# Causal attention and a top-1 expert layer on one core: score tiles cut into quarters of queries, and the expert choice made on the activation instead of in the gate product

## The reference, cut to what matters

```python
x = L0_attn_x                                   # (4, 1024, 128), float32
q, k, v = heads_of(layernorm(x) @ W.T + b)      # 16 heads of 8 columns, for Wq, Wk, Wv
scores = q @ k.T / sqrt(8);  scores = where(causal mask, scores, -9e15)
x = x + softmax(scores) @ v @ Wo.T + bo
z = layernorm(x);  logits = z @ gate_w.T        # 8 experts
sel = argmax(logits);  rw = sigmoid(max(logits))
for e in range(8):
    xs = z * (rw * (sel == e))[:, None]
    out += (xs @ w_up[e].T * silu(xs @ w_gate[e].T)) @ w_down[e].T    # 64 inner columns
return x + out
```

## Time and profile before

| | us |
|---|---|
| median of three runs | 563.52 (563.22 to 566.83) |
| the profiled execution | 562.29 |
| its span | 560.6 |
| front, to the loop's first full unit | 68.64 |
| fifteen units | 341.06 |
| last unit | 24.30 |
| expert steps | 126.60 |

### The profile page before, as it was taken

One profiled execution on the slowest core, in us unless ns is written; L12 is line 12 of the kernel. 1 busy time (PEld: TensorE's weight loads), 2 busy tenths in 40 slices (PEclk: granted clock), 3 DMA queues, 4 the chain that ended last, 5 costly groups with the idle time before them and its releaser, 6 DMA issues.

```text
span 560.6 us, 12273 instructions
## 1 busy us (share of the span) xinstructions
PE 533.4 (95%) x4674; PEld 234.5 (42%) x4674; DVE 449.8 (80%) x668; ACT 385.0 (69%) x771; POOL 211.2 (38%) x393
## 2 busy tenths in 40 slices
PE   8559899999999999999999999999988999999996
PEld 6324434333343333433434334334223555666553
DVE  6938899999999999999999999999924655655631
ACT  7224688898998998988989899899886322222221
POOL 5577264443363444533544346314142111111100
PEclk9769999999999999999999999999999999999999
DMA  6151122320211511102232021120030112121000
GB/s 174 30 168 52 37 64 73 111 66 10 65 37 36 168 28 57 56 18 69 80 104 68 10 66 42 43 69 10 7 100 4 48 56 62 56 58 57 19 20 19
DMA packets 27866, 32.45 MB, mean 58 GB/s; under 512 B 4384, under 2 KB 21280, under 8 KB 27808
## 3 DMA queue, kind: packets, MB, share of 16 engines
q1 hardware_dynamic: 27664, 31.28, 19.2%
q10 hardware_dynamic: 144, 0.39, 0.2%
HBM read 20.26 MB, written 11.01 MB: 56 GB/s over the span
## 4 chain that ended last, share of the span: by engine, by line
PE 70%; DVE 18%; ACT 4%; POOL 3%; issue 2%; DMA 2%; ACTq 1%; POOLq 0%; DVEq 0%
PE ps L1062 19%; PE ps L1046 13%; PE ps L1003 8%; DVE top_p L825 7%; DVE top_p L827 6%; PE ps L1115 6%; PE ps L1123 5%; PE ps L1112 5%; ACT prob L681 4%; DVE top_p L820 3%; PE ps L1013 3%; PE ps L947 2%; PE ps L938 2%; PE ps L1113 2%; PE ps L1021 1%
## 5 line engine op out<-in xcount | busy, mean ns | idle before, releaser
L681 ACT ACTIVATE prob<-ps 128x512 f32<-128x512 f32 (+2 forms) x640 | 307.5, 560 | 41.6 <-PE ps L1046 36.8
L827 DVE TENSOR_REDUCE top_p<-ps 128x2 f32<-128x1024 f32 x192 | 223.6, 1217 | 5.4 <-PE ps L1013 1.8
L1046 PE MATMUL ps<-q_rows,k_rows 51*128 51x512 bf16 (+3 forms) x768 | 168.9, 328 | 2.7 <-ACT prob L681 1.4
L1062 PE MATMUL ps<-prob,v_all 128*9 128x512 f32 (+3 forms) x1536 | 156.8, 488 | 0.7 <-ACT sum_sb L672 0.4
L581 POOL TENSOR_SCALAR_AFFINE_SELECT prob<-prob 128x512 f32<-128x512 f32 x128 | 81.4, 636 | 184.8 <-ACT prob L681 183.0
L1003 PE MATMUL ps<-k_rows,q_rows 48*128 48x512 bf16 (+2 forms) x896 | 130.7, 305 | 8.9 <-DMA k_rows<-split_parts 6.9
L1046 PEld LDWEIGHTS ps<-q_rows,k_rows 51*128 51x128 bf16 x768 | 52.4, 93 | 135.4 <-ACT prob L681 120.0
L825 DVE TENSOR_REDUCE top_p<-ps 128x4 f32<-128x1024 f32 x64 | 76.4, 1214 | 3.5 <-PE ps L1013 3.3
L1003 PEld LDWEIGHTS ps<-k_rows,q_rows 48*128 48x128 bf16 x896 | 42.8, 94 | 45.3 <-issue 15.5
L724 ACT ACTIVATE prob<-ps 128x512 f32<-128x512 f32 x32 | 19.1, 597 | 56.0 <-PE ps L1113 56.0
L903 DVE TENSOR_TENSOR prob<-ps,prob 128x512 f32<-128x512 f32 x32 | 22.1, 690 | 36.9 <-PE ps L1115 36.9
(11 more groups left out here) (90 smaller groups left out, 430.1 us busy)
## 6 DMA issues: line engine op xcount, KB each, us to landing
split_parts<-part SPq DMA_DIRECT2D x6, 768.0 KB, 5.1
q_rows<-split_parts SPq DMA_DIRECT2D x31, 96.0 KB
k_rows<-split_parts SPq DMA_DIRECT2D x31, 96.0 KB
value_sums<-sum_sb SPq DMA_DIRECT2D x128, 18.0 KB
x_sb<-x SPq DMA_DIRECT2D x8, 256.0 KB, 4.5
qk<-value_sums SPq DMA_DIRECT2D x8, 256.0 KB, 3.6
qk<-inverse_sums SPq DMA_DIRECT2D x8, 256.0 KB, 3.8
out<-y SPq DMA_DIRECT2D x8, 256.0 KB, 2.3
```

Of the source, the lines that this page charges most:

```text
L681: a.activation(prob[:, i % NB, g0:g0 + heads, 0:cols], ps[:, load_at(u, n) % 3, 0:heads * cols].rearrange("p (s t) -> p s t", s=heads), AC ...
L827: return v.tensor_reduce(top_p[:, place, qt, s:s + 3:2], banks, AX.X, ALU.max)
L1046: last = mm(ps[:, l % 3, m * cols:(m + 1) * cols], k_rows[rows, k, s + m, j * P:(j + 1) * P], q_rows[rows, k, s + m, c * HALF + q0:(c + 1) ...
L1062: last = mm(ps[32 * g:32 * g + HD + 1, BANK_V, q0:HALF], v_all[:, b, j, first_head + g, :], prob[:, i % NB, g, 0:n], start=(j == 0), stop= ...
```

## The change

Two parts of the program are rewritten.

**The loop.** The eight quarters of 64 tokens in each half of a batch are stored in another order (1, 3, 5, 7, 6, 4, 2, 0, done on the inputs before the launch and undone on the output), keys are put back in their natural order when `xn_t` is written, so q is projected in two products. A query tile is now two quarters that do not adjoin: Y tiles are quarters 1, 3 and 5, 7 of a half, X tiles 6, 4 and 2, 0, and a Z tile is one quarter of each kind, its two halves of 64 queries with different keys. There are 17 pieces per unit. A mask is one matmul per bank instead of two. The queries of a slot are still as many, but lie in the middle of the half, and POOL masks two pieces of 64 columns instead of one of 128. The turn is one transpose (48 columns) instead of four, the join two instructions on 64 partitions each. `send_parts` issues two DMAs instead of one, and stands at another place of SP's queue; the expert weights are loaded during unit 2.

**The expert steps.** The chosen expert's rank is spread over all partitions (PE, then a copy by ACT) and DVE compares and multiplies it into the activation (`choose`, four per step); the `shut` products are gone; gates run ahead of the ups; `down` comes in two parts with the spread rank and the turn between them.

```diff
-PIECES = []
-PIECES.append((P, 0, [(qt, s, P * qt, True) for qt in (0, 4) for s in range(2)]))
...
-PIECES += [(HALF, 2, [(qt, s, 0, False)]) for qt in range(4, 8) for s in range(2)]
+PIECES = [("X", Q, [(c, s, m) for c in range(2) for s in range(2) for m in range(2)], 5)]
+for c in range(2):
+    blocks = [(c, s, m) for s in range(2) for m in range(2)]
+    PIECES += [("Y", P, blocks, 3), ("Z", P, blocks, 4)]
+    PIECES += [("X", 2 * P, [(c, s, 0) for s in range(2)], 6), ("Y", 2 * P, [(c, s, 1) for s in range(2)], 2)]
...
+PIECES += [(tile, HALF, [(1, s, m)], place) for m in range(2) for tile, place in (("X", 7), ("Y", 1))
+           for s in range(2)]
...
-ORDER = "PSSPVSSVaSSPSSPSVSSPVSPSSSPSVSSPSPSVVSPSSPVSPSSVbSSPSPVSSSPVSPSSPSSSPSVS"
+ORDER = "SPSPSSVVaVSSPPSSVSSSPVSSPSSPSSVSPSPSSVSPSVSPSSPVSSbSPSPSVSPSSVSSPSPSVSS"
...
 def send_parts(b, h, units=range(UPB)):
...
+                for s in range(2):
+                    sp.dma_start(split[:, :, UPB * b + units.start:UPB * b + units.stop, :, :, h, s, :]
...
 def step(u, between=None):                       # POOL
-                        blockv = prob[:, i % NB, :, 0:P]
-                        g.affine_select(out=blockv, in_=blockv, pattern=[[0, GH], [1, P]], base=0,
...
+                        for z in range(2):
+                            q0 = (SLOTS[i][3] - Q) * z
+                            quarter = prob[:, i % NB, :, q0:q0 + Q]
+                            last = g.affine_select(out=quarter, in_=quarter, pattern=[[0, GH], [1, Q]],
...
 def copy_xn(b, h):                               # ACT
-                a.activation(xn_t[:, h, :], ps[:, bank, :], ACT.Copy).then_inc(xn_t_set[h], 1)
+                tokens = xn_t[:, h, :].rearrange("p (m e t) -> p m e t", e=2, t=Q)
+                a.activation(tokens[:, :, 1, :], ps[:, bank, 0:HALF // 2].rearrange("p (m t) -> p m t", t=Q), ACT.Copy)
+                a.activation(tokens[:, ::-1, 0, :], ps[:, bank, HALF // 2:].rearrange("p (m t) -> p m t", t=Q),
...
 def join(u, c):                                  # DVE
+                for h in range(2):
+                    rows = slice(Q * h, Q * h + Q)
+                    last = v.tensor_reduce(top[rows, c].rearrange("p g (k m) -> p k g m", k=2),
...
 def route(n, h):                                 # DVE
-                chain.link(v.tensor_reduce(first[:, h, :], hit[:, h], AX.X, ALU.max))
-                v.tensor_tensor(refused[:, h], hit[:, h],
...
+                v.tensor_reduce(rank[:, h, :], hit[:, h], AX.X, ALU.max).then_inc(rank_set, 1)
...
+            def choose(n, h, pr):
+                n_pr = 4 * (n - 1) + pr + 1
+                dve.wait_ge(rank_b_set, n)
+                dve.wait_ge(silu_set, n_pr)
+                v.scalar_tensor_tensor(silu[:, pr % 2, :], rank_b[:, h, :], rank_of[:, pr:pr + 1],
+                                       silu[:, pr % 2, :], ALU.is_equal, ALU.mult).then_inc(chosen_set, 1)
...
 def piece(u, n, r):                              # PE
-                if masked[0]:
-                    for e in range(2):
-                        for rg in range(2):
...
+                        if tile == "Z":
+                            for h in range(2):
+                                q0 = (2 + m) * P if h == 0 else m * P + Q
+                                k0 = (1 - m) * 2 * P + Q if h == 0 else m * 2 * P + P
+                                last = mm(ps[Q * h:Q * h + Q, first_bank + rg, cols],
+                                          q_rows[rows, k, c, s, q0:q0 + Q], k_rows[rows, k, c, s, k0:k0 + P],
+                                          start=(y == 0), stop=False, skip_group_check=True)
+                            continue
...
+                if masked:
+                    for rg in range(2):
...
 for n in range(1, STEPS + 1):                    # PE
-                back(n, n4, h, 0)
+                gate(n, n4, h, 0)
+                gate(n, n4, h, 1)
...
+                down(n, n4, (0, 1))
                 if more:
-                    turn_refused(n + 1, 1 - h)
+                    spread_rank(n + 1, 1 - h)
                     turn_xs(n + 1, 1 - h)
-                down(n, n4)
+                down(n, n4, (2, 3))
```

More of the change, by code:

```diff
@@ L25 @@
 ROWS_M = ROWS + 3
+TOP_COLS = 2 * 3 * 2 * TPH
 INV_COLS = HEADS * SEQ // P
@@ L196, in layer_kernel @@
         hit = sb("hit", [P, 2, TPH, EXPERTS])
-        first = sb("first", [P, 2, TPH])
-        refused = sb("refused", [P, 2, TPH, EXPERTS], BF16)
-        refused_t = sb("refused_t", [EXPERTS, HALF], BF16)
+        rank = sb("rank", [P, 2, TPH], BF16)
+        rank_b = sb("rank_b", [P, 2, HALF])
         weight = sb("weight", [P, 2, TPH])
@@ L377, in step @@
                     send_sums(u - 1, 1)
-                b, k = divmod(u - 1, UPB)
-                if k == 0 and b + 1 < BATCH:
-                    for h in range(2):
-                        send_parts(b + 1, h)
                 if between:
@@ L868, in _ @@
                         take(e)
+            for e in range(EXPERTS):
+                last = v.memset(rank_of[INNER * (e % 2):INNER * (e % 2 + 1), e // 2:e // 2 + 1], float(EXPERTS - e))
+            last.then_inc(rank_of_set, 1)
             def x1_of(b, h):
@@ L1007, in piece @@
[L1007 to L1015 removed]
+                        cols = slice(y * width, (y + 1) * width)
@@ L1200 @@
     r = run_bass_kernel_spmd(nc, [given], core_ids=[0])
-    return r.results[0]["out"]
+    return by_quarter(r.results[0]["out"], [QUARTERS.index(n) for n in range(len(QUARTERS))])
```

331 lines of the change are left out of this document (177 added, 154 removed).

## The result

The changed kernel takes 550.1 us (median of 4 runs, 546.2 to 551.2) against 565.2 us for the kernel before beside it (4 runs, 563.2 to 567.9): **ratio 0.972, 95% interval 0.966 to 0.978**. The forecast was 535.8 us with a range of 525 to 551. The sign holds, and the range by 0.9 us. The size is 15.0 us where 27.7 were forecast, and it comes from the half of the change from which the smaller part was expected. Its profiled execution took 546.21 us, with a span of 544.5; the one of before 562.29 and 560.6.

What follows compares the result with a forecast made beforehand. DVE was taken to bound the loop, PE alone the expert steps. Loop -18.6, last unit +0.3, front +1.0 and expert steps -10.1 sum to -27.4 us from 562.29, hence 534.9 profiled and 535.8 us median, range 525 to 551.

Steps and rivals of the forecast that it cites:

- The bound of the loop: Fifteen units: DVE needs 22.1 us without waits, 97% of the 22.73 us period, and sets it.
- the period is again DVE's, 20.9 us plus waits: Changed loop: 0.6 us of waits kept, period 21.5 us, a gain of 1.24 per unit, -18.6 us over 15.
- the waits grow: Rival in the loop: three engines within 8% of each other wait more and cancel the gain; 544 to 556 us, chance 0.16.
- since ACT and not DVE set it: Loop case: the 341 us stay and only the expert steps gain, 554 us; counted within a chance of 0.16.
- wrong if DVE's idle time per unit exceeds 1.2 us: Sign in the new profile's loop that would make the forecast wrong, one of three such signs.
- The last unit: POOL's two masks of 256 columns for one of 512 show partly in this unit: +0.3 us, bounds 0 to +1.5.
- The front: Before the units: extra DMA issues, ACT instructions and q products +2.0, one piece less -1.0; +1.0 us, bounds -1 to +4.
- The expert steps: Four shut products fewer and a change added, -1.14 us per step, -9.1 for eight; with the end, -10.1 us.
- The tail: End of the expert steps: the first half of down follows the last up at once, 5.69 to 4.7 us, -1.0.
- The cover: Expert step: fourth hidden product ready 10.6 us after the first gate, wanted by down's second half at 12.4; 1.8 us spare.
- The choice held up by POOL: Rival in expert steps: POOL slows DVE's `choose` through shared memory, the step gains only half; 541 us, chance 0.08.

Runs made afterwards that it cites:

- expert_only: The kernel before with only the new expert steps, its loop and front as they were; 549.1 us, ratio 0.972 to the kernel before.
- loop_only: The changed kernel's loop and front with the old expert steps; 566.8 us, ratio 1.002 to the kernel before.
- dve_light: The changed kernel with DVE reducing a unit's eight full-width pieces over half their columns; 547.1 us, period 22.49 us.
- before_dve_light: The kernel before with DVE's twelve full-width reductions of a unit over half their columns; 558.4 us, period 22.46 us.
- pe_light: The changed kernel with each values product of the loop on half its columns; 550.2 us, period 22.03 us.
- best: The changed kernel with turn a one place later, xn's turn behind the first up, and 28 unread products in the last unit; 546.5 us, ratio 0.965 to before.
- join_one: The changed kernel with each join as one instruction on 128 partitions; 549.2 us, ratio 0.972 to the kernel before, period 22.37 us.

## Why the prediction was right and wrong

**The bound of the loop (wrong, and the step that failed).** "Without waits DVE needs 22.1 us, 97% of the period. It is the bound" holds for the kernel before. What followed from it, "the period is again DVE's, 20.9 us plus waits", doesn't. DVE's work did fall to 21.1 us, near the 20.9 of the sum, by 0.85 and not 1.24; of the difference of 0.39, some 0.36 is the two pairs of joins, at +0.33 each where +0.15 was taken. But the period went to 22.50, since a second row stood at 22.46 in the old loop. The prediction had PE at 19.4 us of "its own work" and ACT at 19.4, and took the distance of each from 22.7 for free room. They are not two independent rows: while PE does values ACT gets no new loads (ACT waits 24.7 us for PE in the thirteen periods), and ACT's exponentials leave PE without banks (103.8 us). The sentence that PE stands still for ACT 8 us per unit named the place, and it was used only as the rival "the waits grow". That rival, 544 to 556 with a chance of 0.16, and in it the case "since ACT and not DVE set it", at 554, is nearest to what happened. Of -18.6 us the loop's periods gave -3.1 + 0.8.

**A gain of an engine's work is no gain of the period.** The criterion "wrong if DVE's idle time per unit exceeds 1.2 us" was met, with 1.43.

**The last unit (too small).** +0.3, bounds to +1.5; measured +3.9, of which some 2.7 belong to a clock of 1.2 GHz for 6.8 us, and 1.3, within the bounds, do not. This clock isn't the new loop's: expert_only, with the old loop, was granted 0.75 in the stretch from 406.4 to 440.0 and took 33.7 us for the unit.

**The front (+1.0).** It can't be read from one execution: 65.5 us before, 63.4 after, 67.0 in loop_only and 63.8 in expert_only, with 17.0, 10.2, 13.6 and 13.6 us at 1.2 GHz ahead of 45 us (loop_only has 3.4 more at 50). Among traces with 13.6 us in all, the new front took 64.2 us (`dve_light`) and the old one 63.8 and 64.9 (expert_only, `before_dve_light`): no cost of 1.0 us shows.

**The expert steps (right in mechanism, one term too small).** -10.1 was forecast, -15.7 measured. The shut product was priced by the distance behind it alone, 0.31 us, and costs 0.51 with what it does to its neighbours: 4 x 8 x 0.20 = 6.4 us more. Against that stand 0.3 us per step that the sum hadn't: the wait of 0.32 us for xn. The tail is right: from the last up's start to the down product's end 5.69 us before, 540.60 - 536.01 = 4.59 now, -1.1 for -1.0. The cover was followed through well too: the fourth hidden product was said to be ready 10.6 us after the first gate, and was after 10.56 (489.83, 500.39).

**The choice held up by POOL.** The four choices take 0.74 us each, not 0.65, and nothing waits for them:

```profile
L930 DVE SCALAR_TENSOR_TENSOR prob<-rank_b,rank_of,prob 128x512 f32<-128x512 f32 x32 | 22.8, 742 | 2.0 <-ACT prob L740 1.7
L774 DVE TENSOR_SCALAR xn<-x_sb,moments,rstd 128x128 f32<-128x128 f32 x28 | 12.5, 506 | 10.3 <-POOL rstd L482 10.3
```

The hold is real but falls elsewhere. L774, 342 ns before, is now 506: POOL's addition of 512 columns starts in the same 0.1 us.

```profile
489.86 1.27 POOL L605 TENSOR_TENSOR rest<-qk 128x512 f32<-128x512 f32 x1
```

```profile
489.92 2.06 DVE L774 TENSOR_SCALAR xn<-x_sb,moments,rstd 128x128 f32<-128x128 f32 x4 [1.48 <-POOL rstd L482]
...
517.65 1.12 DVE L774 TENSOR_SCALAR xn<-x_sb,moments,rstd 128x128 f32<-128x128 f32 x4 [1.48 <-POOL rstd L482]
```

At 517.65 no such addition ran beside it, and the four instructions took 1.12 us. The 0.94 us are what PE waits 0.32 us for. The Trainium skill, GPSIMD Engine Reference, Key points, has GpSimd contend with VectorE's instructions that use two ports, by mode or by two inputs; the trace agrees in that this instruction, with a single tensor input, took 2.06 us beside the addition and 1.12 without it. In which mode it ran no run shows.

**Sum of errors.** Loop +16.3, last unit +3.6, front -3.1, expert steps -5.6: +11.2, and the profiled execution came out at 546.2 against 534.9. The median lies another 3.9 above that, the other runs having a mean granted clock of 0.966 to 0.972 against 0.981. The forecast counted 1.2 for this, and added it wrongly: 534.9 + 1.2 is 536.1, not 535.8.

**Luck.** The time lies 0.9 us inside the upper end of the range. The loop alone missed by 16.3 us, and what brought the sum back is the gain of the expert steps, 5.6 us above the forecast because a shut product was priced too low. Without this second error the time would have been 555.7 us, outside the range. That it holds doesn't confirm the account of the loop.

## What to carry to other kernels

Before a saving is multiplied by a loop count, ask how far below the period the next row stands, and measure it where that is possible: leaving out a quarter of the bounding engine's work in the kernel before (half the columns of twelve reductions) shows at once what savings on these instructions can bring together (here 0.28 of 22.74 us). It says nothing of instructions that it leaves as they are, as the join shows. Two engines that hand banks to each other are to be read as one row, with their mutual waits, and not each by its busy share. A small product of another type between large ones is priced by the distance between its neighbours with it and without it, not by its own.

## What the runs showed of the hardware

- **The clock fell inside the loop when PE had less to do.** In pe_light PE was busy about 20 of 22 us per period, and the granted clock went to 1.2 GHz for 3.4 to 13.7 us at a time in five places between 100 and 400 us; the changed kernel has none there. The period that it hit hardest in this stretch took 25.2 us:

```profile
135.00:160.20 25.20, 23.48 (x249) 7.76 (x247) 21.29 (x24) 19.63 (x42) 10.41 (x26) 0.73 0.14 39
160.20:182.20 22.00, 19.83 (x265) 7.74 (x260) 20.83 (x23) 20.42 (x44) 11.45 (x28) 1.00 0.30 81
```

  So work taken from PE came back as time: the run took 550.2 us, no less than the changed kernel.
- **One program spreads over 4 to 6 us**, and this goes with its mean granted clock. In the traces, that of pe_light apart, the stretches at 1.2 GHz lie in the front, the first period, the last unit and at the very end. The kernel before took 562.3 at 0.982 and 567.4 at 0.970, best 541.0 at 0.987 and 547.2 at 0.970.
- **Half the partitions, no shorter:** a join of 64 elements lasts 259 ns on 64 partitions and 264 on 128 (join_one).
